# A fused scan and expert kernel: tiles and steps placed one by one, and the batch loop written out

## The reference, cut to what matters

```python
x = L0_attn_x                                  # (16, 512, 512): batch, time, channel
xn = _layernorm(x)
# branch 1: selective scan, 16 states for each channel
x_dbl = einsum('bld,kd->blk', xn, x_proj_w)    # -> delta_un (128), B (16), C (16)
delta = softplus(einsum('blr,dr->bld', delta_un, dt_proj_w) + dt_proj_b)
state = exp(delta*A) * state + delta*B*xn      # along time, for each channel and state n
y = sum_n state * C;  s = y + xn * D_param
# branch 2: eight experts, top 2 of a gate, biases, relu, mean of the two, then silu
g = silu(mean over the top 2 of relu(xn @ expert_w[e] + expert_b[e]))
out = x + s * g
```

## Time and profile before

| | |
|---|---|
| time, median of 3 runs | 2230.43 us (2226.74 to 2242.84) |
| the profiled execution's own time | 2227.24 us |
| its span | 2225.5 us |
| PE busy | 1810.6 us, 81% |
| DVE busy | 1962.6 us, 88% |
| ACT busy | 1369.2 us, 62% |
| POOL busy | 1881.8 us, 85% |
| moved by the DMA engines | 641.23 MB, mean 288 GB/s |

### The profile page before, as it was taken

One profiled execution on the slowest core, in us unless ns is written; L12 is line 12 of the kernel. 1 busy time (PEld: TensorE's weight loads), 2 busy tenths in 40 slices (PEclk: granted clock), 3 DMA queues, 4 the chain that ended last, 5 costly groups with the idle time before them and its releaser, 6 DMA issues.

```text
span 2225.5 us, 34699 instructions
## 1 busy us (share of the span) xinstructions
PE 1810.6 (81%) x8688; PEld 1177.6 (53%) x8688; DVE 1962.6 (88%) x3114; ACT 1369.2 (62%) x2370; POOL 1881.8 (85%) x1112
## 2 busy tenths in 40 slices
PE   4597987978789797887969879697896978879886
PEld 2364655545555464555646556365554655546554
DVE  4688899898898988899888998989988898998997
ACT  3456567666566665666565666656665666665664
POOL 2867998888889887898878988788897888988896
PEclk8799999999899999998989999999998999999997
DMA  5869798897969989699797987879888897897995
GB/s 227 287 223 373 231 334 306 255 345 245 355 223 295 330 252 353 222 308 326 244 348 223 324 310 255 328 240 342 276 272 317 256 357 247 295 332 243 374 291 161
DMA packets 279396, 641.23 MB, mean 288 GB/s; under 512 B 22272, under 2 KB 22784, under 8 KB 268944
## 3 DMA queue, kind: packets, MB, share of 16 engines
q1 hardware_dynamic: 185776, 446.36, 57.4%
q10 hardware_dynamic: 68832, 125.34, 15.7%
q0 software_dynamic: 24576, 67.13, 10.9%
HBM read 516.58 MB, written 122.16 MB: 287 GB/s over the span
## 4 chain that ended last, share of the span: by engine, by line
PE 30%; DVE 26%; issue 19%; POOL 10%; ACT 8%; DMA 3%; ACTq 2%; DVEq 1%; SPq 0%; POOLq 0%
PE z_ps L1102 15%; DVE scan_ps L944 11%; POOL dbx L501 6%; DVE p_sb L954 5%; DVE h_sb L944 4%; PE proj_ps L1052 4%; PE y_ps L1118 3%; ACT scan_ps L654 3%; PE y_ps L1135 2%; POOL pp_sb L512 2%; PE xt_ps L1087 2%; DMA c_sb<-bc_rows 2%; PE proj_ps L1078 1%; ACT r_sb L675 1%; ACTq L691 1%
## 5 line engine op out<-in xcount | busy, mean ns | idle before, releaser
L501 POOL TENSOR_TENSOR dbx<-b_sb,u_sb 128x1024 f32<-128x1024 f32 x512 | 1240.8, 2552 | 122.7 <-DMA b_sb<-bc_rows 59.8
L1102 PE MATMUL z_ps<-w_sb,xsT 128*128 128x512 f32 x1920 | 900.4, 613 | 109.3 <-ACT r_sb L675 109.3
L654 ACT ACTIVATE scan_ps<-delta,a_sb 128x512 f32<-128x512 f32 x1024 | 700.1, 690 | 431.1 <-DVE p_sb L954 374.1
L944 DVE TENSOR_TENSOR_SCAN scan_ps<-scan_ps,dbx 128x512 f32<-128x512 f32 x704 | 847.1, 1218 | 104.4 <-ACT scan_ps L654 73.7
L1102 PEld LDWEIGHTS z_ps<-w_sb,xsT 128*128 128x128 f32 x1920 | 356.7, 196 | 490.1 <-issue 474.7
L1118 PE MATMUL y_ps<-ident,p_sb 128*128 128x128 f32 x2816 | 422.8, 284 | 153.8 <-DVE p_sb L954 153.5
L512 POOL TENSOR_TENSOR pp_sb<-h_sb,c_sb 128x1024 f32<-128x1024 f32 (+1 forms) x192 | 410.8, 2139 | 148.2 <-PE y_ps L1135 74.1
L1118 PEld LDWEIGHTS y_ps<-ident,p_sb 128*128 128x128 f32 x2816 | 337.7, 145 | 296.9 <-DVE p_sb L954 212.0
L954 DVE TENSOR_TENSOR p_sb<-scan_ps,c_sb 128x512 f32<-128x512 f32 x704 | 473.5, 673 | 1.3 <-PE y_ps L1118 1.1
L944 DVE TENSOR_TENSOR_SCAN h_sb<-scan_ps,dbx 128x512 f32<-128x512 f32 x320 | 388.1, 1213 | 82.3 <-ACT scan_ps L654 80.5
L669 ACT ACTIVATE xsT<-xt_ps 128x512 f32<-128x512 f32 x240 | 141.7, 590 | 89.3 <-issue 46.5
(11 more groups left out here) (117 smaller groups left out, 1385.7 us busy)
## 6 DMA issues: line engine op xcount, KB each, us to landing
w_sb<-in_ew SPq DMA_DIRECT2D x240, 1024.0 KB, 7.3
b_sb<-bc_rows SPq DMA_DIRECT2D x64, 1024.0 KB, 12.0
ys_rows<-r_sb ACTq DMA_DIRECT2D x240, 256.0 KB, 5.7
xs<-xs_rows ACTq DMA_DIRECT2D x238, 256.0 KB
c_sb<-bc_rows SPq DMA_DIRECT2D x64, 512.0 KB, 14.7
xn<-in_x SPq DMA_DIRECT2D x16, 1024.0 KB, 16.6
c_sb<-bc_rows SPq DMA_DIRECT2D x16, 1024.0 KB, 18.0
xo<-in_x SPq DMA_DIRECT2D x64, 256.0 KB, 8.0
```

The source lines that it names most:

```text
L501: nc.gpsimd.tensor_tensor(dbx[:, k % DBX_PAIRS], b_sb[:, 2 * m:2 * m + 2, :], u_sb[:, dt % 2, :].unsqueeze(1).to_broadcast([P, 2, T]), ALU ...
L654: nc.scalar.activation(scan_ps[:, bank_of(j), :], delta[:, dt % 2, :], ACT.Exp, scale=a_sb[:, dt, n:n + 1]).then_inc(da_ready, 1)
L944: nc.vector.tensor_tensor_scan(state, bank, dbx[:, j // 2 % DBX_PAIRS, r % 2, :], 0.0, ALU.mult, ALU.add).then_inc(scanned, 1)
L1102: nc.tensor.matmul(z_ps[:], xsT[:, slot, c, :], w_sb[:, i % WRING, c, :], start=(c == 0), stop=False)
```

## The change

The tables of unit numbers are set anew, the three constant lags are replaced by tables of their own, and the loop goes.

- `TILE_AT`: units 8, 11, 15, 18, 22, 26, 29, 33, 36, 40, 44, 47, 51, 54, 58 become 6, 9, 12, 16, 20, 25, 30, 34, 37, 41, 44, 48, 51, 55, 59. `RELU_LAG` becomes 6, and 7 for tiles at units 16 to 34.
- `STEPS`: NX1 26 to 27, Z3 28 to 30, NK 35 to 38, NR 41 to 43, NS 42 to 45, NZ0 48 to 50. Copies: Z1 6 to 7, NX0 30 to 31, NX1 32 to 34, Z3 34 to 38, NR 47 to 48, NS 48 to 50, NZ0 54 to 56. Delta is stored one to four units later (Z1 11, Z2 20, Z3 42, NZ0 60). DVE forms u one unit after the copy's first part: Z1 8, Z2 16, Z3 39, NZ0 57.
- `FRONT`: the apply steps at 11, 14, 15, 16, the gate at 34 (32), the rank at 41 (38). The sigmoids, `XD_AT` and `COPY_Y_AT` move by a unit in places.
- `over_batches` writes all 16 batches out.

```diff
-STEPS = {0: "Z1", 9: "Z2", 16: "NT0", 18: "NT1", 20: "NT2", 22: "NT3", 24: "NX0", 26: "NX1", 28: "Z3",
-         35: "NK", 41: "NR", 42: "NS", 48: "NZ0"}
+STEPS = {0: "Z1", 9: "Z2", 16: "NT0", 18: "NT1", 20: "NT2", 22: "NT3", 24: "NX0", 27: "NX1", 30: "Z3",
+         38: "NK", 43: "NR", 45: "NS", 50: "NZ0"}
...
-COPY_LAG = 6
-DELTA_LAG = 10
-DVE_LAG = 7
-
-FRONT = {"stats": (2, 3, 4, 5), "var": 5, "root": 8, "apply": (11, 13, 13, 15), "gate": 32, "rank": 38}
+COPY_AT = {7: "Z1", 15: "Z2", 22: "NT0", 24: "NT1", 26: "NT2", 28: "NT3", 31: "NX0", 34: "NX1", 38: "Z3",
+           48: "NR", 50: "NS", 56: "NZ0"}
+FIRST_COPY_AT = {7: "Z1", 15: "Z2", 27: "NT0", 29: "NT1", 31: "NT2", 33: "NT3", 35: "NX0", 37: "NX1", 39: "Z3",
+                 51: "NR", 52: "NS", 56: "NZ0"}
+DELTA_AT = {11: "Z1", 20: "Z2", 42: "Z3", 60: "NZ0"}
+FIRST_DELTA_AT = {11: "Z1", 20: "Z2", 43: "Z3", 60: "NZ0"}
+
+FRONT = {"stats": (2, 3, 4, 5), "var": 5, "root": 8, "apply": (11, 14, 15, 16), "gate": 34, "rank": 41}
...
-TILE_AT = {8 + (i * 36) // 10: i for i in range(TILES)}
+TILE_AT = {j: i for i, j in enumerate((6, 9, 12, 16, 20, 25, 30, 34, 37, 41, 44, 48, 51, 55, 59))}
...
-RELU_LAG = 7
+
+RELU_LAG = 6
+BUSY_UNITS = range(16, 35)
 
 LOAD_LAG = EVAC_LAG
-STORE_LAG = RELU_LAG + 1
+STORE_LAG = 1
...
-COPY_Y_AT = {24: 0, 41: 1, 56: 2, 8: 3}
-SIG_AT = ((27, 28, 29), (43, 44, 45), (57, 58, 59), (9, 11, 12))
+COPY_Y_AT = {24: 0, 41: 1, 56: 2, 9: 3}
+SIG_AT = ((28, 29, 30), (43, 44, 46), (57, 58, 59), (10, 11, 12))
...
+        def relus_at(b):
+            return {j + RELU_LAG + (j in BUSY_UNITS): i for j, i in tiles_at(b).items()}
...
-        def over_batches(eng, body):
-            body(0, 0, 0)
-            body(1, 1, 0)
-            with eng.Fori(1, B // 2 - 1) as i:
-                body(i * 2, 0, i)
-                body(i * 2 + 1, 1, i)
-            body(B - 2, 0, B // 2 - 1)
-            body(B - 1, 1, B // 2 - 1)
+        def over_batches(body):
+            for b in range(B):
+                body(b, b % 2, b // 2)
...
-                    name = steps.get(j - COPY_LAG)
+                    name = copies.get(j)
...
-                    name = steps.get(j - DELTA_LAG)
+                    name = deltas.get(j)
...
-                    if j - RELU_LAG in tiles:
-                        tile_relu(b, par, pair, tiles[j - RELU_LAG])
+                    if j in relus:
+                        tile_relu(b, par, pair, relus[j])
...
-                    name = steps.get(j - DVE_LAG)
+                    name = copies.get(j - 1)
```

More of the change, by code:

```diff
@@ L29 @@
 ORDER = list(STEPS.values())
-COPY_LAG = 6
-DELTA_LAG = 10
-DVE_LAG = 7
-FRONT = {"stats": (2, 3, 4, 5), "var": 5, "root": 8, "apply": (11, 13, 13, 15), "gate": 32, "rank": 38}
+COPY_AT = {7: "Z1", 15: "Z2", 22: "NT0", 24: "NT1", 26: "NT2", 28: "NT3", 31: "NX0", 34: "NX1", 38: "Z3",
[5 more added lines that the diff above has]
+FRONT = {"stats": (2, 3, 4, 5), "var": 5, "root": 8, "apply": (11, 14, 15, 16), "gate": 34, "rank": 41}
 FIRST_FRONT = {"stats": (11, 11, 12, 12), "var": 13, "root": 16, "apply": (19, 19, 20, 20), "gate": 37, "rank": 44}
-XD_AT = {62: 0, 7: 1, 31: 2, 46: 3}
+XD_AT = {62: 0, 6: 1, 31: 2, 47: 3}
 XD_ADD_AT = 1
@@ L260, in tiles_at, with relus_before, copies_at, deltas_at @@
             return FIRST_TILE_AT if is_first(b) else LAST_TILE_AT if is_last(b) else TILE_AT
-        def tiles_before(b):
-            return {} if is_first(b) else FIRST_TILE_AT if is_second(b) else TILE_AT
+        def relus_at(b):
+            return {j + RELU_LAG + (j in BUSY_UNITS): i for j, i in tiles_at(b).items()}
+        def relus_before(b):
+            return {} if is_first(b) else relus_at(b - 1)
+        def copies_at(b):
+            return FIRST_COPY_AT if is_first(b) else COPY_AT
+        def deltas_at(b):
+            return FIRST_DELTA_AT if is_first(b) else DELTA_AT
         def sig_at(b):
@@ L572, in batch @@
                         gather_first(b, par, pair, range(TT))
-            over_batches(pool, batch)
+            over_batches(batch)
             for q in (QUADS - 2, QUADS - 1):
@@ L731, in batch @@
                 nxt = not is_last(b)
-                steps, front, sig = steps_at(b), front_at(b), sig_at(b)
-                tiles, before = tiles_at(b), tiles_before(b)
+                front, sig = front_at(b), sig_at(b)
+                tiles, relus, before = tiles_at(b), relus_at(b), relus_before(b)
+                copies, deltas = copies_at(b), deltas_at(b)
                 for j in range(UNITS):
@@ L738, in batch @@
                         load_rows(b + 1, 1 - par, ROWS_AT.index(j))
-                    if j - STORE_LAG in tiles:
-                        store_rows(b, par, tiles[j - STORE_LAG])
+                    if j - STORE_LAG in relus:
+                        store_rows(b, par, relus[j - STORE_LAG])
                     if j - STORE_LAG + UNITS in before:
@@ L759, in batch @@
                     for part in range(3):
-                        name = steps.get(j - COPY_LAG - part)
+                        name = copies.get(j - part)
                         if name == "NZ0" and nxt:
@@ L775, in batch @@
                         keep_turned(b, par, tiles[j - EVAC_LAG])
-                    if j - RELU_LAG in tiles:
-                        tile_relu(b, par, pair, tiles[j - RELU_LAG])
-                    if j - RELU_LAG + UNITS in before:
-                        tile_relu(b - 1, 1 - par, pair if par else pair - 1, before[j - RELU_LAG + UNITS])
+                    if j in relus:
+                        tile_relu(b, par, pair, relus[j])
+                    if j + UNITS in before:
+                        tile_relu(b - 1, 1 - par, pair if par else pair - 1, before[j + UNITS])
                     if j in COPY_Y_AT:
@@ L793, in batch @@
                     da_unit(b, j)
-            over_batches(act, batch)
+            over_batches(batch)
             copy_y(B - 1, 1, DT - 1)
@@ L996, in batch @@
                 nxt = not is_last(b)
-                steps, front, sig = steps_at(b), front_at(b), sig_at(b)
+                copies, front, sig = copies_at(b), front_at(b), sig_at(b)
                 for j in range(UNITS):
@@ L1027, in batch @@
                         times_c(b - 1, UNITS - 1)
-            over_batches(dve, batch)
+            over_batches(batch)
             times_c(B - 1, UNITS - 1)
@@ L1181, in batch @@
                             add_y_quad(b - 1, q + QUADS)
-            over_batches(pe, batch)
+            over_batches(batch)
             for q in (QUADS - 2, QUADS - 1):
```

## The result

| | before | after |
|---|---|---|
| median of the runs, us | 2231.8 | 2304.1 (2300.7 to 2311.1) |
| ratio, 95% interval | | 1.032 [1.027, 1.037] |
| span of the profiled execution, us | 2225.5 | 2298.9 |
| mean granted clock of TensorE | 0.949 | 0.919 |
| DVE busy, us | 1962.6 | 2004.2 |

The change made the kernel 3.2% slower. The forecast was 2155 us (2115 to 2205).

What follows compares the result with a forecast made beforehand. Bound: a round of transfers, POOL's work and DVE's work with waits on late PE, plus loop back edges. 2227.2 less 31 (loop) less 14 x 3 = 42 gives 2154, said as 2155 us (2115 to 2205).

Steps and rivals of the forecast that it cites:

- No loop: Batches 3 to 12: taking away the loop's five back edges, 6.3 us each, saves 31 us (19 to 37).
- Tiles and steps of the middle: Middle of batches 1 to 14: PE less crowded, 3 us (1 to 4.5) of DVE's 5.7 us waits go.
- The round: Batch 13's closed chain of 133.1 us: transfers 44.5, POOL's work 38.4, DVE's work with waits 50.2.
- third part: From unit 28 to SP's next write: 50.2 us of DVE's work with 5.7 us of waits; 3 us to go.
- middle part: From POOL's first product with C to unit 28: 38.4 us of POOL's work.
- DVE busy 122 as before: Sign to check in a middle batch of about 129.5 us: DVE's busy time stays at 122 us.
- Rank at 41: Rank three units later, with POOL's scatter waiting for it: costs nothing, at most a unit, 2 us.
- Relus: Relus one unit earlier, early tiles three units apart: nothing, covered by ACT's lead; without it up to 2.9 us.
- B and C rows: NR, NS, NZ0 later: SP's write of these rows does not shift, at worst a unit, 2 us a batch.
- (d): Rival: early relus make ACT wait for unfinished tiles, two 2.9 us waits a batch, 81 us, 2277 us; chance 0.05.
- (e): Rival: looser spacing lowers the matrix clock for the four middle tiles, 58 us lost, 2254 us; chance 0.02.

Runs made afterwards that it cites:

- e10: Changed kernel with PE's transposition of rows one unit earlier for the tiles at 25 and 30 alone: 2295.0 us, ratio 1.027.
- e14: Changed kernel with e10's earlier transpositions, e3's comparisons, and tiles from 34 on back at their old units (33 to 58): 2225.9 us, ratio 0.997.
- e3: Changed kernel with the gate's eight comparisons as another operation, taking one operand from PSUM in place of SBUF: 2316.0 us, ratio 1.038.
- e6: Changed kernel with the old tile units, every relu seven units later, and e3's comparisons: 2204.0 us, ratio 0.988.
- e12: Changed kernel with every relu seven units after its tile, new tile units kept: 2317.2 us, ratio 1.039.
- e13: Changed kernel with the old tile units, the new relu lags and e3's comparisons: 2197.9 us, ratio 0.983.

## Why the prediction was wrong

**No loop**: right. 31 us forecast, 27 measured, and its rows show the same (no "issue", batches of one length).

**Tiles and steps of the middle**: this step failed. It put 14 x 3 = 42 us into the sum as a gain; all new tables together lost 101. "PE gets back some 8 us by unit 29, which is what it was late by" counted how much work PE has by a unit, and ACT does not wait for an amount. It waits for one transposition with a fixed place (e10: with that one a unit sooner and PE's work the same, the waits ahead of 26 and 31 are gone), ahead of the tile in between when tiles are four units apart and behind it when they are five. The step said of a wait in rows 4 that ACT's "own load of rows waits there for a transposition on PE", and did not ask where the transposition goes with the new gaps. The 3.4 us that were to go became 4.00 and 5.25. Where that is mended (e14), the forecast gain is there, 2.7 us at unit 30, and the waits at NX1, which the text expected as 2 to 3 us "late next", and behind the tile at 30 take it back. Taking 3 us of 5.7 assumed that the two would not be equal.

**The round**: "Only waits in the third part shorten the round" was drawn up for gains. The middle part, "38.4 us of POOL's work", had room to grow and grew to 44.2, with new waits ahead of 21 and 26 (0.98 and 3.35 us, means of batches 3 to 12) that lay outside the part I looked at; the one ahead of 24 shrank from 1.92 to 1.01. The third part, which was to shrink by 3 us, grew by 1.6.

**"DVE busy 122 as before"**: wrong, 125.1. The sum moved the gate by two units at no cost. Its cover was POOL's 4.5 us of idleness, which I had read only as something to be gained. POOL still waits 4.68 us for PE in the kernel after, but DVE now comes to the gate later than that. This term is 3.1 us a batch in the kernel after, 42 in all, but taking it away was worth between -12 and 60 us, by what else DVE meets behind it (e3, e6).

**Last tile at 59**: the part-by-part does not name it, so it counts as nothing; 3 to 14 us. **Rank at 41**: taken as nothing, "at most a unit"; DVE waits 1.4 us a batch for the counts there, whose worth no run shows.

**Relus, B and C rows**: right as terms of the sum. Lag 6 does not cost over the whole (e12, and e13 against e6: 6 us less), and the part from the write to the product is 43.6 us (44.5).

**The rivals.** (d) had the right sign and a wrong cause: its wait is there, 2.18 us ahead of unit 57, but a lag of 7 does not make the kernel faster. (e) is partly true: the four middle tiles ran at 1.00 in the kernel after, but the clock fell elsewhere, with PE waiting more. None had the rows' order or the shared port. A chance of 0.05 for slower came from giving doubt only to the sizes of a gain; a table in which some thirty entries move had as many ways to lose.

## What to carry to other kernels

With engines in order, a place in a table means "behind everything that my engine meets before", so for each moved step read who stands ahead of it, and what that one waits for: one unit was 5.5 us on PE. An engine's idle time in the profile can be cover for another's operation, so check which operations of DVE run while POOL is idle before that time is filled. And when single fixes give nothing, try two together: here edits that gave -9 and +12 us by themselves gave -53 together.

## What was not expected of the hardware

- A comparison of 128x9 numbers from SBUF to SBUF, 0.22 us of work, stood 3.3 us behind POOL's products, and up to 5.8 in e10, through the boundary between two of them. As another operation with its first operand in PSUM it took 0.22 us beside POOL, although it still read one operand from SBUF.
- A loop's back edge on four engines cost 5.4 us (27 us over five), in a kernel with the same tables and work.
- TensorE's clock, in the same stretch of the same kernel, was at 0.50 in one batch and at 1.00 in the next (e3), and the two lasted 143.7 and 139.5 us.
